# One VectorE instruction of 1024 columns instead of two of 512, for du and for silu, in a selective-scan kernel

## What is computed

```python
z = einsum(mz, Wc) + bc                       # folded into one matrix here
dlt, Bm, Cm = split(einsum(z, Wdbc))
delta = softplus(einsum(dlt, Wdt) + bdt)
dA  = exp(delta[..., None] * A)               # 16 states
dBu = delta[..., None] * Bm[:, :, None, :] * z[..., None]
h = dA_t * h + dBu_t                          # scan over the tokens
y = einsum('ben,bn->be', h, C_t) + z * Dp
out = (silu(mx) * y_forward + silu(mx) * flip(y_backward)) @ Wf ...
```

## Time and profile before

| what | value |
|---|---|
| median of 3 runs | 3286.95 us (3286.11 to 3287.86) |
| the profiled execution's own time | 3287.22 us |
| its span in the trace | 3285.4 us |
| DVE busy | 3025.4 us, 92% |
| PE busy | 3000.4 us, 91% |
| POOL busy | 2904.5 us, 88% |
| ACT busy | 2690.6 us, 82% |

### The profile page before, as it was taken

How to read it: one execution, slowest core, us unless ns; L and a number is a source line. 1 busy time by engine, 2 the same in 40 slices (tenths; PEclk the granted TensorE clock), 3 DMA queues, 4 the chain that set the end, 5 groups by cost and what they waited for, 6 DMA issues and landing times.

```text
span 3285.4 us, 54883 instructions
## 1 busy us (share of the span) xinstructions
PE 3000.4 (91%) x19924; PEld 2380.0 (72%) x19924; DVE 3025.4 (92%) x2008; ACT 2690.6 (82%) x5151; POOL 2904.5 (88%) x1288
## 2 busy tenths in 40 slices
PE   8887999899998999899999999899999999899999
PEld 5766666667677666678778676678778666677789
DVE  2838999999999999999999999999999999999994
ACT  1448999988888999987888999987878999988772
POOL 1528999999999999999999999999999999999993
PEclk9989999999999999999999999999999999999999
DMA  5765334644475334645565334645566333645563
GB/s 222 245 237 175 132 117 137 227 154 163 162 249 205 130 119 135 222 139 167 166 229 201 128 122 136 225 142 162 166 211 220 122 128 130 232 136 163 157 198 111
DMA packets 207054, 560.40 MB, mean 171 GB/s; under 512 B 20201, under 2 KB 66473, under 8 KB 202561
## 3 DMA queue, kind: packets, MB, share of 16 engines
q1 hardware_dynamic: 203424, 538.01, 49.0%
q0 software_dynamic: 2304, 16.78, 1.4%
q10 hardware_dynamic: 1056, 2.10, 0.2%
HBM read 476.19 MB, written 80.63 MB: 169 GB/s over the span
## 4 chain that ended last, share of the span: by engine, by line
PE 41%; ACT 21%; DVE 19%; issue 11%; POOL 1%; DVEq 0%; ACTq 0%; POOLq 0%
PE y L888 12%; DVE hbuf L1326 10%; PE slot L899 8%; ACT abuf L1134 8%; PE mb L969 6%; PE mb L859 5%; DVE slot L1326 5%; ACT slot L1195 4%; PE slot L911 3%; ACT dec L1195 3%; DVE delta L1260 2%; DVE hbuf L1331 2%; PE mb L869 1%; ACT soft L1090 1%; ACT yrd L1125 1%
## 5 line engine op out<-in xcount | busy, mean ns | idle before, releaser
L1239 POOL TENSOR_TENSOR hbuf<-hbuf,cres 128x1024 f32<-128x1024 f32 x704 | 1666.4, 2382 | 145.0 <-DVE hbuf L1326 143.7
L1234 POOL TENSOR_TENSOR bst<-bst,du 128x1024 f32<-128x1024 f32 x512 | 1224.6, 2392 | 47.2 <-DVE du L1270 47.2
L1326 DVE TENSOR_TENSOR_SCAN hbuf<-dec,slot 128x1024 f32<-128x1024 f32 x512 | 1164.8, 2275 | 38.5 <-PE slot L911 25.5
L888 PE MATMUL y<-ident,hbuf 128*128 128x128 f32 x8192 | 1017.8, 273 | 1.7 <-POOL hbuf L1239 1.7
L888 PEld LDWEIGHTS y<-ident,hbuf 128*128 128x128 f32 x8192 | 926.2, 141 | 106.0 <-issue 103.4
L1134 ACT ACTIVATE abuf<-dut,bt 128x128 f32<-128x128 f32 x3072 | 970.6, 390 | 0.0
L1326 DVE TENSOR_TENSOR_SCAN slot<-slot,bst 128x1024 f32<-128x1024 f32 x320 | 728.0, 2275 | 24.1 <-ACT slot L1195 23.1
L1195 ACT ACTIVATE dec<-delta,par 128x1024 f32<-128x1024 f32 x512 | 586.3, 1145 | 185.3 <-DVE hbuf L1326 184.8
L1195 ACT ACTIVATE slot<-delta,par 128x1024 f32<-128x1024 f32 x512 | 568.1, 1110 | 123.3 <-DVE hbuf L1331 110.9
L859 PE MATMUL mb<-xn,wzs 128*128 128x512 f32 x1008 | 478.8, 597 | 58.1 <-DVE delta L1260 43.6
L899 PEld LDWEIGHTS slot<-ident,abuf 128*128 128x128 f32 x3072 | 339.4, 141 | 218.3 <-ACT abuf L1134 131.1
(11 more groups left out here) (157 smaller groups left out, 2306.3 us busy)
## 6 DMA issues: line engine op xcount, KB each, us to landing
bst<-bc_s SPq DMA_DIRECT2D x512, 512.0 KB, 3.9
cres<-bc_s SPq DMA_DIRECT2D x128, 512.0 KB, 6.7
wzs<-wz_s SPq DMA_DIRECT2D x64, 256.0 KB, 4.1
yf_s<-yrd SPq DMA_DIRECT2D x32, 512.0 KB, 5.4
ybuf<-yf_s SPq DMA_DIRECT2D x32, 512.0 KB, 5.0
yg_s<-ybuf SPq DMA_DIRECT2D x31, 512.0 KB, 4.4
si_s<-silu SPq DMA_DIRECT2D x28, 512.0 KB, 6.1
silu<-si_s SPq DMA_DIRECT2D x28, 512.0 KB, 5.4
```

Of the source, the lines that this page charges most:

```text
L888: last = nc.tensor.matmul(y[:, j * P:(j + 1) * P], hbuf[:, q % HR, j * P:(j + 1) * P], ident[:], start=False, stop=(q % N == N - 1), is_tr ...
L1234: nc.gpsimd.tensor_tensor(bst[:, i % BR, :], bst[:, i % BR, :], du[:, k % 2, :], ALU.mult).then_inc(pool_b, 1)
L1239: nc.gpsimd.tensor_tensor(hbuf[:, q % HR, :], hbuf[:, q % HR, :], cres[:, q % N, :], ALU.mult).then_inc(pool_prod, 1)
L1326: nc.vector.tensor_tensor_scan(h[:, ::step], decays[:, ::step], inflows[:, ::step], 0.0, ALU.mult, ALU.add).then_inc(scanned, 1)
```

## The change

`du` of all 1024 columns is made by one instruction, `inflow_factor`, after the scan of step zs+4. `turn_du` of the first half therefore moves from step zs+4 to zs+5 in every unit; the second stays at zs+6. `silu` is made by one instruction, `make_silu`, after step 1 of the next unit, where the second half was; the one after step 15 is gone. The semaphores `du_ready` and `silu_ready` count one where they counted two, so whoever waited for a first half waits for the whole. `turn_b` and `copy_bt` move from step zs+4 to zs-1, and `z_part` waits for the copy. The orders of SP and POOL are unchanged, and ACT's but for `copy_bt`.

```diff
             def turn_b(g):
                 bank = mb[0] if g > 0 else slot[1]
-                if g > 0:
-                    pe.wait_ge(du_ready, 2 * ET * g + 1)
+                if g > 0 and gates(ET * g - 1):
+                    pe.wait_ge(gated, pair(ET * g - 2) + 1)
+                elif g > 0:
+                    pe.wait_ge(delta_ready, ET * g + 1)
...
             def turn_du(k, h):
-                pe.wait_ge(du_ready, 2 * k + h + 1)
-                if h == 0 and k % ET == 0 and k > 0:
-                    pe.wait_ge(bt_ready, k // ET + 1)
+                pe.wait_ge(du_ready, k + 1)
...
+                        if c == zs - 1 and new_b:
+                            turn_b((k + 1) // ET)
                         if zs <= c < zs + 4:
                             z_part(k + 1, (c - zs) // 2, range((c - zs) % 2 * 2, (c - zs) % 2 * 2 + 2))
-                        if c == zs + 4 and new_b:
-                            turn_b((k + 1) // ET)
-                        if c == (zs + 5 if new_b else zs + 4):
+                        if c == zs + 5:
                             turn_du(k + 1, 0)
...
-            def inflow_half(k, h):
+            def inflow_factor(k):
                 f = wtile(k)
-                dve.wait_ge(ud_ready, 2 * k + h + 1)
+                dve.wait_ge(ud_ready, 2 * k + 2)
...
-                nc.vector.scalar_tensor_tensor(out=du[:, k % 2, half(h)], in0=z_bank(k, h),
+                nc.vector.scalar_tensor_tensor(out=du[:, k % 2, :], in0=z_tile(k),
                                                scalar=par[:, f // ET, f % ET, PBZ:PBZ + 1],
-                                               in1=delta[:, k % 2, half(h)], op0=ALU.add, op1=ALU.mult).then_inc(du_ready, 1)
...
+            def make_silu(k):
+                dve.wait_ge(sig_ready, 2 * mx_index(k) + 2)
+                stored = k // (2 * ET) * (ET - 1) + (ET - 1 if backward(k) else k % ET - 1)
+                if stored > 0:
+                    dve.wait_ge(si_out, 16 * stored)
+                nc.vector.scalar_tensor_tensor(out=silu[:], in0=mbw[:], scalar=par[:, 1, k % ET, PBX:PBX + 1],
+                                               in1=soft[:], op0=ALU.add, op1=ALU.mult).then_inc(silu_ready, 1)
...
                         if has_mx(k - 1):
-                            silu_half(k - 1, 1)
+                            make_silu(k - 1)
...
-                    if c in (zs + 2, zs + 4) and k + 1 < NU:
-                        inflow_half(k + 1, (c - zs - 2) // 2)
-                    if c == 15 and has_mx(k):
-                        silu_half(k, 0)
+                    if c == zs + 4 and k + 1 < NU:
+                        inflow_factor(k + 1)
```

More of the change, by code:

```diff
@@ L614, in dbc_job, with z_tile @@
             return k - ET - 1 if ET < k < ET + 1 + NC - 2 else None
+        def z_tile(k):
+            return mbw[:] if k > 0 else y[:]
         def z_bank(k, h):
-            return mb[h] if k > 0 else y[:, half(h)]
+            return z_tile(k)[:, half(h)]
         def wait_scanned_out(eng, q):
@@ L800, in _ @@
                     if c == 5 and k > 0 and has_mx(k - 1) and not backward(k - 1):
-                        sp.wait_ge(silu_ready, 2 * mx_index(k - 1) + 2)
+                        sp.wait_ge(silu_ready, mx_index(k - 1) + 1)
                         sp.dma_start(scratch["si"][pair(k - 1)], silu[:]).then_inc(si_out, 16)
@@ L840, in delta_product @@
                     if k >= 2 and has_mx(k - 2):
-                        pe.wait_ge(silu_ready, 2 * mx_index(k - 2) + h + 1)
+                        pe.wait_ge(silu_ready, mx_index(k - 2) + 1)
                     elif k >= 2 and dbc_job(k - 2) is not None:
@@ L857, in z_part @@
                         pe.wait_ge(delta_ready, k + 1)
+                    if h == 0 and k > 0 and k % ET == 0:
+                        pe.wait_ge(bt_ready, k // ET + 1)
                 for i in ks:
@@ L878, in skip_terms @@
                 else:
-                    pe.wait_ge(du_ready, 2)
+                    pe.wait_ge(du_ready, 1)
                 for j in range(ET):
@@ L1087, in softplus_start @@
                 if k >= 2 and has_mx(k - 2):
-                    act.wait_ge(silu_ready, 2 * mx_index(k - 2) + 2)
+                    act.wait_ge(silu_ready, mx_index(k - 2) + 1)
                 act.wait_ge(dps_mm, 2 * k + 2)
@@ L1232, in inflow @@
                 pool.wait_ge(b_in[i % BR], 16 * (i // BR + 1))
-                pool.wait_ge(du_ready, 2 * k + 2)
+                pool.wait_ge(du_ready, k + 1)
                 nc.gpsimd.tensor_tensor(bst[:, i % BR, :], bst[:, i % BR, :], du[:, k % 2, :], ALU.mult).then_inc(pool_b, 1)
@@ L1269, in inflow_half @@
                     dve.wait_ge(dut_mm, 2 * (k - 1))
-                nc.vector.scalar_tensor_tensor(out=du[:, k % 2, half(h)], in0=z_bank(k, h),
+                nc.vector.scalar_tensor_tensor(out=du[:, k % 2, :], in0=z_tile(k),
                                                scalar=par[:, f // ET, f % ET, PBZ:PBZ + 1],
-                                               in1=delta[:, k % 2, half(h)], op0=ALU.add, op1=ALU.mult).then_inc(du_ready, 1)
[L1274 to L1282, removed]
+                                               in1=delta[:, k % 2, :], op0=ALU.add, op1=ALU.mult).then_inc(du_ready, 1)
+            def make_silu(k):
[5 more added lines that the diff above has]
+                                               in1=soft[:], op0=ALU.add, op1=ALU.mult).then_inc(silu_ready, 1)
             def gate_y(k):
@@ L1288, in gate_y @@
                 else:
-                    dve.wait_ge(silu_ready, 2 * mx_index(k) + 2)
+                    dve.wait_ge(silu_ready, mx_index(k) + 1)
                 bank = mbw if k < NU - 1 else slot[0]
@@ L1307, in _ @@
             finish_delta(0)
-            for h in range(2):
-                inflow_half(0, h)
+            inflow_factor(0)
             for k in range(NU):
```

## The result

The changed kernel takes 3381.89 us (median of 4 runs, 3380.3 to 3384.8) against 3286.53 for the kernel before in the same comparison: ratio 1.0287, 95% interval 1.0274 to 1.0300, so about 95 us slower. The forecast was 3364, its range 3305 to 3405.

The account below looks back on a forecast made before the run. The prediction took DVE to set a unit's pace up to du and PE from there to the scan of step 0. Terms of 39.8, 29.7, 5.6 and 1.5, together 76.6 us, on 3287.2 gave 3364 us, range 3305 to 3405.

Parts of the forecast that it names:

- PE sets the end of a unit: From du to the scan of step 0, PE's unbroken work sets the pace; DVE's saving of 0.15 a unit gains nothing.
- The rival that DVE's busy time decides: PE's lateness vanishes in spare time and DVE's savings stay: 15 us faster, 3264 to 3272; chance 0.09.
- The late du, mx units: PE waits for whole du, so the inflow of step 14 and the chain behind come 0.94 us later per unit.
- The silu, mx units: Silu moved from after step 15 to after step 1, where no DVE wait hides it: 0.48 us more per unit.
- Both in one unit: Late du and moved silu added in each mx unit: 28 x (0.94 + 0.48) = 39.8 us.
- the fourth rival: PE's clock falls after its longer waits, costing 1.5 us per mx unit: up to 3406; chance 0.11 for 3388 and more.
- The late du, projecting units: Projection, `spread_inflow` and the scan of step 0 come 1.10 us late; same price for units with `make_dbc`.
- The boundaries: At seven changes of direction, moved `turn_b` waits for delta or the gating at zs-1: 0.8 us each, between 0 and 2.
- DVE busy 23 us less: Sign expected in the profile: merging the halves of du and silu cuts DVE's busy time by some 23 us.

Follow-up runs that it names:

- pad_end: The changed kernel with one more DVE instruction per unit, behind step 15, whose result no one reads; 3384.91 us, ratio 1.0288 to the kernel before.
- halves_late: The kernel before with both halves of du made after the scan of step zs+4 and the first `turn_du` at zs+5; 3334.46 us, ratio 1.0142.
- tuned: The kernel before with one projection tile moved behind step 0 and ACT's scaling of step 2's second half behind step 1's decay; 3270.04 us, ratio 0.9945.
- silu_only: The kernel before with silu made whole after step 1, du and `turn_b` unchanged; 3308.21 us, ratio 1.0050.
- du_only: The changed kernel with silu left in halves as before, so du whole and `turn_b` moved; 3352.97 us, ratio 1.0189 to the kernel before.
- order_only: The kernel before, du still in halves, with only `turn_du` of the first half moved from step zs+4 to zs+5; 3300.96 us, ratio 1.0033.

## Why the prediction was right, and where its sizes were off

- **PE sets the end of a unit.** Right: pad_end, halves_late, and the projecting units of tuned, where DVE's wait only moves along PE's row of work. The gain of tuned in the mx units is another one, by ACT's decay at step 1. The rival that DVE's busy time decides is out: pad_end has 30 us more of it and costs nothing that can be told, silu_only has less and is slower, tuned has as much as before and is faster. One reading went too far: of the 42 waits for L911 only 29 stand at the scan of step 0, all in units without silu, and 13 at step 4, 11 of these behind the slow clock. In the mx units of before none is seen, since the first silu fills it, as the prediction says itself.
- **The late du, mx units.** 0.94 forecast; 0.90 in du_only. PE's wait was 1.1 from start to start, as forecast, with du 0.05 longer and the signal faster (du ends at 1146.20, PE starts at 1146.25, where 0.1 was taken). The gap before the inflow of step 14 took some 0.2 of it back, as forecast: mx to inflow 1.97 before, 1.74 now (1148.06 to 1149.80).
- **The silu, mx units.** 0.48 forecast; 0.53 in silu_only, the half of a tenth by which it is longer.
- **Both in one unit.** 1.42 forecast; 1.45 in the units where PE keeps its clock, 1.60 on average (44.8 / 28). The difference is the fourth rival, in part: with silu whole, PE waits about 1.57 at `delta_product`, and in 19 of 28 units the clock then falls for step 4, against 10 before. I had the mechanism, but left it out of the sum; and where I gave each fall 1.5 us, it cost 0.1 to 0.55, since DVE's scan waits only for the end of the stretch. That it is the clock is read from the durations, the granted clock and the lengths of the units; no edit held the clock, so it isn't shown by one.
- **The late du, projecting units.** 1.10 forecast; 1.14. PE's wait was 0.67 from start to start, where the working gives 0.66. The working counts the projection from the end of du and so has the whole delay; order_only shows that 0.43 of it comes with the new place in the order even when du is ready, since PE stood waiting for ACT's tiles where it used to transpose.
- **The boundaries.** This is the term that was mis-sized: 7 x 0.8 = 5.6 forecast, 15.3 measured, and three of the seven above the upper bound of 2. "The rows don't price that" was true of the wait, but the price lay in what stands behind it: where the clock fell, z at half of it and DVE 2.88 late; where it didn't, 0.9. Putting `turn_b` back behind du (b_late) takes 8 away there and costs 5 at the other three. Why the clock falls at one boundary and not at the next stays open.
- **DVE busy 23 us less.** Wrong as the page counts it: 1.5. The two groups fell by 19, the durations of all by 16.6.
- Together: mx +5, boundaries +10, start, set-up and tail some +3, the rest -1, which makes the 16.5 us between the forecast's sum of 76.6 and the span's 93.1.

## What to carry to other kernels

An instruction that produces for another engine in pieces is also a schedule: merging the pieces saves its own fixed cost and moves the first piece's consumer behind the last one. Before merging, look in the trace for the consumer's place: where its starts join up and it ends the unit, the delay comes through almost in full (0.90 of 1.09 us here), and the producer's saving doesn't. And of two places for the same work, the one in which its engine waits anyway is free: the half of silu at the end of a unit cost nothing, and after step 1 each 0.1 us of it counted.

## What was not expected of the hardware

Two stretches alike in PE's waits, 1.56 and 1.57 us before four matmuls and 0.24 behind them, were followed once by a granted clock of 0.52 and once by full speed (3.62 and 2.02 us for the same 16 matmuls): the wait alone doesn't tell whether the clock falls. The boundaries say the same: behind waits of 2.38 and 2.45 us the mean clock of 14 us was 0.76 once and 1.00 once. And one VectorE instruction of 1024 columns took 1.26 us as du and 1.28 as silu, where delta, with the same sizes but a constant instead of a column as its scalar and other operations, took 1.21; which of these makes the difference wasn't tested.
